# A graph network on one core: the first edge loop re-staged, and a row copy by three 16-bit products

## What is computed

```python
h = relu(layernorm(x)); hw = h @ W.T                     # layer 0, per node
att = leaky_relu(score_src[src] + score_dst[dst])        # per edge and head
x = x + segment_sum(att * hw[src], dst)
h = relu(layernorm(x))                                   # layer 1
z = concat([h[row], h[col], edge_attr]) @ [W_weight, W_gate] + bias
x = x + segment_sum(relu(z_message) * sigmoid(z_gate), row)   # row = src, col = dst
```

## Time and profile before

| what | value |
|---|---|
| time, median of three runs | 5444.96 us (5443.28 to 5455.56) |
| span of the profiled execution | 6861.6 us |
| gather loop in the profile, with its lead-in | 224 to 3233 us |
| second pass over the nodes | 3233 to 3360 us |
| scatter loop in the profile | 3360 to 5950 us |
| third edge loop and final sums | 5950 to 6862 us |

### The profile page before, as it was taken

How to read it: one execution, slowest core, us unless ns; L and a number is a source line. 1 busy time by engine, 2 the same in 40 slices (tenths; PEclk the granted TensorE clock), 3 DMA queues, 4 the chain that set the end, 5 groups by cost and what they waited for, 6 DMA issues and landing times.

```text
span 6861.6 us, 115174 instructions
## 1 busy us (share of the span) xinstructions
PE 4604.1 (67%) x31443; PEld 3550.2 (52%) x31443; DVE 3197.0 (47%) x6951; ACT 1985.4 (29%) x4132; POOL 3725.5 (54%) x3908
## 2 busy tenths in 40 slices
PE   6355555555555555555888878788877878688883
PEld 3244444444444433444566666666666666566663
DVE  7455555555555555566511111112111112399996
ACT  3011111111111111112522222222222222388883
POOL 5654555555555555462366666666666666544442
PEclk8666676676667766677988888888888888899997
DMA  4222222222222222222644444444444444599998
GB/s 144 50 54 50 56 54 53 50 55 52 53 52 54 53 51 52 52 59 56 230 138 138 136 137 137 139 136 140 136 138 137 137 138 141 183 323 325 326 323 313
DMA packets 457998, 866.29 MB, mean 126 GB/s; under 512 B 122766, under 2 KB 276056, under 8 KB 457700
## 3 DMA queue, kind: packets, MB, share of 16 engines
q1 hardware_dynamic: 215031, 439.00, 21.0%
q0 software_dynamic: 177312, 379.95, 19.8%
q10 hardware_dynamic: 65620, 46.95, 2.1%
HBM read 558.92 MB, written 313.00 MB: 127 GB/s over the span
## 4 chain that ended last, share of the span: by engine, by line
PE 39%; issue 19%; DVE 18%; another core or an unknown queue 15%; DMA 6%; ACT 1%; DVEq 1%; SPq 1%; ACTq 0%; POOL 0%; POOLq 0%
PE ps L842 13%; PE ps L840 13%; DMA rows<-parts 5%; PE ps L827 3%; DVE msg L1443 3%; DVE hot L1333 3%; DVE to_node L1317 3%; PE ps L764 2%; PE ps L707 2%; DVE gat L1548 1%; PE ps L675 1%; DVE run_parts L1425 1%; DVE picked L1413 1%; PE ps L720 1%
## 5 line engine op out<-in xcount | busy, mean ns | idle before, releaser
L602 POOL DMA_INDIRECT parts<-rows,sidx x1664 | 1640.5, 986 | 952.9 <-issue 510.6
L1313 DVE TENSOR_SCALAR to_edge<-ps,iota_p 128x1024 bf16<-128x1024 f32 (+1 forms) x417 | 535.3, 1284 | 2084.1 <-remote 1726.7
L842 PE MATMUL ps<-nodes_w,to_edge 128*128 128x256 f32 x3328 | 1117.5, 411 | 231.1 <-issue 226.0
L840 PE MATMUL ps<-w_edge,gat 128*128 128x256 f32 x3328 | 1108.4, 407 | 217.6 <-issue 212.6
L584 POOL DMA_INDIRECT gat<-table,sidx x832 | 859.7, 1033 | 715.9 <-DVE sidx L1325 466.4
L764 PE MATMUL ps<-msg,to_node 128*128 128x128 f32 x3328 | 691.2, 367 | 827.0 <-issue 535.6
L584 POOL DMA_INDIRECT rows<-table,sidx x832 | 793.5, 954 | 663.8 <-DVE sidx L1325 388.2
L764 PEld LDWEIGHTS ps<-msg,to_node 128*128 128x128 f32 x3328 | 609.0, 270 | 883.7 <-issue 883.1
L840 PEld LDWEIGHTS ps<-w_edge,gat 128*128 128x128 f32 x3328 | 675.1, 204 | 431.2 <-issue 328.5
L842 PEld LDWEIGHTS ps<-nodes_w,to_edge 128*128 128x128 f32 x3328 | 677.0, 205 | 416.0 <-issue 324.7
L1044 ACT ACTIVATE rows<-ps 128x512 f32<-128x512 f32 x832 | 466.7, 604 | 1385.8 <-remote 694.8
(11 more groups left out here) (231 smaller groups left out, 6574.3 us busy)
## 6 DMA issues: line engine op xcount, KB each, us to landing
rows<-parts SPq DMA_DIRECT2D x208, 1028.0 KB, 7.5
ea<-in_edge_attr SPq DMA_DIRECT2D x422, 256.0 KB
nodes_w<-table_b SPq DMA_DIRECT2D x208, 128.0 KB
parts<-rows,sidx POOLq DMA_INDIRECT x1664
nodes_w<-table_a SPq DMA_DIRECT2D x416, 64.0 KB, 5.1
gat<-table,sidx POOLq DMA_INDIRECT x832
rows<-table,sidx POOLq DMA_INDIRECT x832
x1w<-x ACTq DMA_DIRECT2D x208, 64.0 KB
```

Of the source, the lines that this page charges most:

```text
L602: nc.gpsimd.indirect_dma_start(out=parts, out_offset=bass.IndirectOffsetOnAxis(ap=sidx[:, s, j:j + 1], axis=0), in_=rows[:, s, j, :], in_o ...
L840: pe.matmul(z, eat[:, s % 2, j // 4, (j % 4) * P:(j % 4 + 1) * P], w_edge[:], start=True, stop=False)
L842: mmi = pe.matmul(z, to_edge[:, s % 2, j * P:(j + 1) * P], nodes_w[:, s, :], start=False, stop=True)
L1313: return nc.vector.tensor_scalar(to, spread.rearrange("p b n -> p (b n)"), iota_p[:], None, ALU.is_equal)
```

## The change

In the first edge loop TensorE's step q takes the work of one step in two halves. Ahead of a wait for `dve0` (VectorE has reduced the scores of group q) stand `turn_keys(q)` and `find_places(q - 1)`, behind it `sum_messages(q - 1)`, `expand_scores(q + 1)`, `spread_rel` and `match_keys(q)`. The places go to the free half of bank 7, where the counts are. VectorE's step q makes the messages of group q itself (before: q - 1), and adds the sums of q - 2 (before: q - 1). ScalarE's queue stores the window of q - 2 at the start of step q and loads that of q - 1 behind its first two evictions. In the scatter loop the window of `table_b` is cut, two steps ahead, into three bf16 parts that add up to it (ScalarE makes the first and the second, VectorE the rest and the third), the one-hot matrix is written in bf16, and three bf16 products take the place of the fp32 one.

```diff
-        SCORES = F + J * B
+        SCORES = F
+        places = ps[:, 7, J * B:2 * J * B]
...
+        b_parts = hot[:, :, 0:3 * 2 * F].rearrange("p s (k f) -> p s k f", k=3)
+        b_rest = hot_t[:].rearrange("p a j n -> p (a j n)").bitcast(F32)[:, 0:2 * 2 * F].rearrange("p (r f) -> p r f", r=2)
+        to_edge_h = [to_edge[:, k, :].bitcast(BF16)[:, 0:GE] for k in range(2)]
...
                 pe.wait_ge(earlier_up, 2 * q + 2)
                 for j in range(J):
-                    at = ps[:, 4, F + j * B:F + (j + 1) * B]
+                    at = places[:, j * B:(j + 1) * B]
                     pe.matmul(at, hot_t[:, s % 2, j, :], digits[:, s % 2, j, :], start=True, stop=False)
                     mmi = pe.matmul(at, earlier[:, j, :], ones_b[:], start=False, stop=True)
-                return mmi
+                mmi.then_inc(places_ps, 1)
...
             def sum_messages(s, q):
                 pe.wait_ge(to_node0, q + 1)
                 pe.wait_ge(copied0, q + 2)
-                pe.wait_ge(msgs0, q + 1)
-                out_ps = ps[:, 4, 0:F]
                 for j in range(J):
-                    mmi = pe.matmul(out_ps, to_node[:, s % 2, j * P:(j + 1) * P],
+                    mmi = pe.matmul(ps[:, 4, 0:F], to_node[:, s % 2, j * P:(j + 1) * P],
                                     msg[:, s % 2, j * F:(j + 1) * F], start=(j == 0), stop=(j == J - 1))
+                return mmi
+
+            def expand_scores(s, q, turn):
+                pe.wait_ge(to_edge_up[0], q + 1)
+                pe.wait_ge(sdw_in[s], 16 * (turn + 1))
+                for j in range(J):
+                    mmi = pe.matmul(ps[:, 4, SCORES + j * 3 * HEADS:SCORES + (j + 1) * 3 * HEADS],
+                                    to_edge_b[:, j * P:(j + 1) * P], sdw[:, s, :], start=True, stop=True)
+                mmi.then_inc(expanded, 1)
...
-            def by_dst_step(s, q, i, turn, w, first):
-
+            def by_dst_step(s, q, i, turn, first, last):
+                pe.wait_ge(digits_up, q + 1)
+                pe.wait_ge(picked_up, q + 1)
+                turn_keys(s, q)
                 if s > 0 or not first:
-                    pe.wait_ge(digits_up, q)
-                    turn_keys((s - 1) % U, q - 1)
-                    sum_messages((s - 1) % U, q - 1)
-                    if s > 1 or not first:
-                        pe.wait_ge(picked_up, q)
-                        find_places((s - 2) % U, q - 2)
-                pe.wait_ge(to_edge_up[0], q + 1)
-                pe.wait_ge(sdw_in[s], 16 * (turn + 1))
...
-                spread_rel(0, i, s + 1)
+                    find_places((s - 1) % U, q - 1)
+                pe.wait_ge(dve0, 3 * q + 1)
                 if s > 0 or not first:
-                    match_keys((s - 1) % U, q - 1)
+                    summed = sum_messages((s - 1) % U, q - 1)
+                    if last and s == U - 1:
+                        summed.then_inc(last_ps, 1)
+                if s < U - 1 or not last:
+                    expand_scores((s + 1) % U, q + 1, turn if s < U - 1 else turn + 1)
+                if s < U - 2 or not last:
+                    spread_rel(0, i, s + 2)
+                match_keys(s, q)
...
-            def edge_products(s, q, f, i, turn):
+            def edge_products(s, q, f, i):
                 pe.wait_ge(to_edge_up[1], f + 1)
                 spread_rel(1, i, s + 1)
-                pe.wait_ge(bw_in[s], 16 * (turn + 1))
+                pe.wait_ge(part_act, 2 * q + 2)
+                pe.wait_ge(part_dve, 2 * q + 2)
                 pe.wait_ge(ea_t, 2 * q + 4)
                 for k in range(4):
                     pe.wait_ge(part_up, 4 * q + k + 1)
...
                         z = ps[:, 4 + k, (j % 2) * 2 * F:(j % 2 + 1) * 2 * F]
                         pe.matmul(z, eat[:, s % 2, j // 4, (j % 4) * P:(j % 4 + 1) * P], w_edge[:],
                                   start=True, stop=False)
-                        mmi = pe.matmul(z, to_edge[:, s % 2, j * P:(j + 1) * P], nodes_w[:, s, :],
-                                        start=False, stop=True)
+                        for part in range(3):
+                            mmi = pe.matmul(z, to_edge_h[s % 2][:, j * P:(j + 1) * P], b_parts[:, s, part, :],
+                                            start=False, stop=(part == 2))
...
+            def store_window(q, g):
+                act.wait_ge(copied0, q + 3)
...
+                act.dma_start(x1[bass.ds(first, P), :], x1o[:]).then_inc(x1_st, 16)
+
+            def load_window(q, g):
+                act.wait_ge(x1_st, 16 * (q + 1))
...
+                act.dma_start(x1w[:], x1[bass.ds(first, P), :]).then_inc(x1_in, 16)
+
+            def by_dst_step(s, q, g, first):
+                if s > 1 or not first:
+                    store_window(q - 2, g - 2)
...
+                if s > 0 or not first:
+                    load_window(q - 1, g - 1)
...
+            def first_part(s, q, turn):
+                act.wait_ge(bw_in[s], 16 * (turn + 1))
+                nc.scalar.activation(b_parts[:, s, 0, :], nodes_w[:, s, :], ACT.Copy).then_inc(part_act, 1)
+
+            def second_part(s, q):
+                act.wait_ge(part_dve, 2 * q + 1)
+                nc.scalar.activation(b_parts[:, s, 1, :], b_rest[:, s % 2, :], ACT.Copy).then_inc(part_act, 1)
+
+            def evict_rows(s, q, turn, last):
+                ahead = s < U - 2 or not last
+                if ahead:
+                    first_part((s + 2) % U, q + 2, turn if s < U - 2 else turn + 1)
...
+                    if k == 1 and ahead:
+                        second_part((s + 2) % U, q + 2)
...
+                dve.wait_ge(places_ps, q + 1)
+                dve.wait_ge(pos_up, q + 1)
...
-            def by_dst_step(v, q, g, turn, w, first):
-
-                f = q + w
+            def by_dst_step(v, q, g, turn, w, first, last):
                 s = v % U
-                last = v > 0 or not first
-                if last:
-                    messages((v - 1) % V, q - 1, turn if v > 0 else turn - 1)
-                    dve.wait_ge(msgs0, q)
-                    next_gather((v - 1) % V, g - 1 + V)
-                dve.wait_ge(spread_up[0], f + 1)
-                by_node(to_edge_b).then_inc(to_edge_up[0], 1)
-                relative(0, dst_of(g + 1), g + 1, s + 1)
-                if last:
-                    dve.wait_ge(keys_ps, q)
-                    split_run((s - 1) % U, q - 1, w)
-                one_hot(s, g).then_inc(hot_up, 1)
-                dve.wait_ge(rel_up[0], f + 1)
-                dve.wait_ge(copied0, q + 1)
+                dve.wait_ge(expanded, U + q + 1)
+                if v > 1 or not first:
+                    add_sums(q - 2)
+                messages(v, q, turn)
+                dve.wait_ge(msgs0, q + 1)
+                next_gather(v, g + V)
+                if v < V - 1 or not last:
+                    dve.wait_ge(spread_up[0], q + 2)
+                    by_node(to_edge_b).then_inc(to_edge_up[0], 1)
+                    relative(0, dst_of(g + 1), g + 1, s + 1)
+                dve.wait_ge(keys_ps, q + 1)
+                if v > 0 or not first:
+                    dve.wait_ge(places_ps, q)
+                split_run(s, q, w)
+                if v > 0 or not first:
+                    pick((s - 1) % U, q - 1, g - 1)
+                if v < V - 1 or not last:
+                    one_hot((s + 1) % U, g + 1).then_inc(hot_up, 1)
+                dve.wait_ge(rel_up[0], q + 1)
                 by_edge(s, iota_ps).then_inc(to_node0, 1)
...
+                for k in range(2):
+                    dve.wait_ge(last_ps, 2 * w + k + 1)
+                    add_sums(q - 2 + k)
...
+            def first_rest(s, q, turn):
+                dve.wait_ge(bw_in[s], 16 * (turn + 1))
+                dve.wait_ge(part_act, 2 * q + 1)
+                nc.vector.tensor_tensor(b_rest[:, s % 2, :], nodes_w[:, s, :], b_parts[:, s, 0, :],
+                                        ALU.subtract).then_inc(part_dve, 1)
+
+            def third_part(s, q):
+                dve.wait_ge(part_act, 2 * q + 2)
+                nc.vector.tensor_tensor(b_parts[:, s, 2, :], b_rest[:, s % 2, :], b_parts[:, s, 1, :],
+                                        ALU.subtract).then_inc(part_dve, 1)
...
+                if ahead:
+                    dve.wait_ge(part_dve, 2 * q + 4)
+                    first_rest((s + 2) % U, q + 2, turn if s < U - 2 else turn + 1)
+                dve.wait_ge(spread_up[1], f + 2)
+                dve.wait_ge(z1_up, 4 * U + 4 * q)
+                by_node(to_edge_h[(s + 1) % 2]).then_inc(to_edge_up[1], 1)
+                if ahead:
+                    third_part((s + 2) % U, q + 2)
```

More of the change, by code:

```diff
@@ L1054, in _ @@
                         evict_turned(s + 1, q + 1)
-                        evict_rows(s, q, turn)
+                        evict_rows(s, q, turn, False)
                 turn = act.snap(w * GU + GU - 1)
@@ new lines, in scatter_step @@
```

(28 more changed lines are left out.)

138 lines of the change are left out of this document (56 added, 82 removed).

## The result

| | before | changed |
|---|---|---|
| median | 5447.22 us (20 runs) | 5456.19 us (20 runs) |
| lowest | 5442.25 us | 5446.23 us |
| highest | 5455.56 us | 5501.94 us |

The ratio is 1.0018, with a 95% interval of 1.0010 to 1.0025: the changed kernel is some 9 us slower (5 to 14), less than the 0.2% that the prediction named as the limit of what can be told. It is inside the range, 5 us above the predicted 5451.

What follows compares the result with a forecast made beforehand. GpSimd's indirect DMAs were taken to bound both edge loops, hiding the rest; 4.1 us at the gather loop's end plus 2.2 at the scatter loop's start made 6.3 on 5445, so 5451 us, range 5439 to 5467.

Steps and rivals of the forecast that it cites:

- GpSimd's pace: Both edge loops: GpSimd's indirect DMAs set the timed pace, 10.1 us a gather step, 10.3 a scatter step; chance 0.83.
- the uncovered ends: Gather loop's end and scatter loop's start, not hidden by GpSimd: together +6.3 us, bounds +1 to +13.
- The bound: Both edge loops: GpSimd paces them; VectorE needs 8.2 us a gather step, TensorE 8.3 a scatter step, 7.4 after the change.
- The rebuilt 5461 or 5493 us: Whole kernel before, rebuilt as if GpSimd never waited; the higher sum counts the first gather's long 65.8 us; 5445 was measured.
- The re-staged loop, the parts, the products: nothing: Both edge loops: new order, copies and subtractions, and bf16 products (0.32 us for three) hidden under GpSimd's pace, priced nothing.
- The end of the gather loop: +4.1: Last scores to SyncE's next DMA: 13.0 us for 8.9, by a second addition, load and store; +4.1 us, bounds 1.3 and 8.
- The start of the scatter loop: +2.2: First product waits for the parts of group 0, so GpSimd's first scatter is 2.2 us later; bounds 0 and 5.
- TensorE as the bound of the scatter loop: Scatter loop: TensorE, not GpSimd, is last, so the products save 183 us, 5262 us; chance 0.08.
- TensorE's issue by records: Timed loops go by TensorE's instruction records, 84 to 100 a scatter step: 408 us slower, 5853 us; chance 0.05.
- VectorE's subtractions: Scatter loop: two-operand SBUF subtractions block GpSimd for their full length, +179 us, 5631 us; chance 0.04.
- by the page it would be 5631: Scatter loop: the skill page on SBUF contention, read as VectorE's two-input subtractions holding up GpSimd's indirect DMAs, giving 5631 us.
- the profiled loop could grow to 3083 us: Profiled scatter loop: if the stalls are the recording's and go by records, from 2590 up to 3083 us, the time unchanged.

Runs made afterwards that it cites:

- e5: Kernel before with GpSimd relieved: five of eight gathers a step, four plain DMAs in place of eight scatters, so work is left out; 4698.53 us, ratio 0.8626.
- e6: Changed kernel with GpSimd relieved: five of eight gathers a step, four plain DMAs in place of eight scatters, so work is left out; 4521.81 us, ratio 0.8303.
- the second recording: The kernel before, unedited, profiled once more; ratio 0.9998 (0.9989 to 1.0007), span 5451.7 us.
- e2: Kernel before with the re-staged first loop alone, the scatter loop keeping the fp32 product; ratio 1.0015 (1.0006 to 1.0024).
- e3: Kernel before with the parts and three bf16 products alone, the first loop as before; ratio 1.0003 (0.9994 to 1.0012).
- e4: Changed kernel with the sums of group 206 added right behind split_run of group 207, ahead of the last two picks; ratio 1.0014 (1.0005 to 1.0023).
- e11: e4 with ScalarE reading the window's index into its register ahead of the wait, for store and load of x1; ratio 1.0012 (1.0003 to 1.0021).
- e7: Kernel before with four more 128x256 fp32 subtractions a step on VectorE in the scatter loop, both operands in SBUF; ratio 1.0067 (1.0050 to 1.0084).
- e8: Kernel before with a one-operand 128x416 reduction, then a two-operand 128x1024 fp32 subtraction, added each scatter-loop step on VectorE; ratio 1.0228 (1.0211 to 1.0245).
- e10: Changed kernel with a one-operand 128x416 reduction on VectorE behind the second subtraction of each scatter-loop step; ratio 1.0019 (1.0010 to 1.0029).

## Why the prediction came out as it did

The mechanism is the one that was forecast, GpSimd's pace over both loops and the loss at the uncovered ends. Three terms were off in size, and partly cancel.

**The bound.** Shown right: GpSimd's pace in both loops, gathers on average 1.254 to 1.259 us apart and scatters 1.288 to 1.292 in every undisturbed recording of a kernel with eight DMAs a step and nothing added on VectorE; and e5 and e6 show the next bounds where the prediction put them (8.2 us for VectorE; 8.3 and 7.4 for TensorE against 8.20 and 7.39). The rebuilt 5461 or 5493 us were high because the rows of the stalled recording were: the first slot at 243.1 in place of 229.1, and the first gather's 65.8 us, 1.1 in the changed kernel. With 229.1 the same sum is 5447, the measured median, but that it fits so well is in part luck. Beside the 5451.7 us of the second recording the sum has the last scores 7 us late (1.26 us a gather for 1.254), the way from there to the first scatter 2 us short, the scatters 3 us long, and the last stretch, which moves by 15 us between recordings, 13 us short.

**The re-staged loop, the parts, the products: nothing.** Right for the loop and the products: e2's gathers take 0.2 us more in all than those of before, and in e6 three bf16 products take 0.33 us (3002.07 to 3002.40) where the sum had 0.32. The parts are not quite nothing: the scatters take 1.5 us longer than before, and 1.1 of it are the 12 collisions with the subtractions (1.1 of 1.8 in e3, 1.9 of 2.5 in e4).

**The end of the gather loop: +4.1.** This term was mis-sized: +5.9. The place and the mechanism were right. To the first addition it is 7.0 us where the sum had 6.5. From there to the load's issue it is 3.4 us where the sum had 2.4, the load takes 1.8 to the second addition for 1.7, and from that to SyncE's DMA it is 2.8 for 2.4: 1.9 us more in all, 14.9 for 13.0. The sum took its 2.4 us from the earlier trace rows, where ScalarE had the window's index in its register and issued the store 0.68 us behind the addition (0.32 in the second recording). In the changed kernel ScalarE reads the index behind the wait, and the issue comes after 1.06 us, twice, and once more it reads it ahead of the load. e11 shows 0.53 us of that for one store.

**The start of the scatter loop: +2.2.** Mis-sized the other way: +1.0 in the changed kernel, +1.5 in e3. The kernel before takes 6.9 us here in the second recording and not 6.35 as in the first. A copy into bf16 is 0.42 us and not 0.36, a smaller error against it.

Together +5.9 and +1.0, +1.5 in the scatters, and -0.9 in a node pass that no edit touches: 7.5 us between the two traces up to the last scatter (the gathers start 0.4 us later and take 0.4 less), where 6.3 were predicted and 9 (5 to 14) measured. The two mis-sized ends, +1.8 and -1.2, partly cancel in the predicted sum.

**The rivals.** TensorE as the bound of the scatter loop: out, e3 gives 1.0003 and not 0.966; e5 and e6 show that it becomes true where GpSimd is relieved, with steps of 8.20 and 7.39 us. TensorE's issue by records: out, by the two spans. VectorE's subtractions: the mechanism that the prediction gave 0.04 exists, the price of 179 us doesn't. (On the 5445 us that the other rivals start from it would be 5624, not 5631.) The argument against it was a row that could not decide: in the earlier trace rows L1425 ends at 1089.93, 0.10 us behind the gather's start, and 0.10 is less than the 0.12 from which a remainder costs. Another pair of the same recording would have shown it:

```profile
2945.41 0.42 DVE L1425 TENSOR_TENSOR run_parts<-run,masks 128x256 int32<-128x256 int32 x1
...
2945.59 1.08 POOL L584 DMA_INDIRECT rows<-table,sidx  x1 [0.30 <-issue]
```

With 0.24 us left the gather takes 1.08 us and not 0.96; it is the longest of its line in the earlier trace rows. In the second recording of before 21 gathers start with more than 0.13 us of L1425 left, and 19 take longer, by up to 0.22. The change escapes by its place: its second subtraction ends at 3403.60 and the next scatter starts at 3403.83 (timeline of the changed kernel):

```profile
3402.54 0.98 POOL L607 DMA_INDIRECT parts<-rows,sidx  x1 [0.30 <-ACT rows L1081]
3403.19 0.41 DVE L1553 TENSOR_TENSOR hot<-hot_t,hot 128x256 bf16<-128x256 f32 x1
...
3403.83 0.98 POOL L607 DMA_INDIRECT parts<-rows,sidx  x1 [0.30 <-issue]
```

VectorE is released by the landing of a scatter (1453 us of its idle time in the loop end with one), so it stands in step with GpSimd, and in nearly every step the subtractions fall in the same place. The Trainium skill, "SBUF — State Buffer", § Who interferes with whom, says that the order of issue and not the shape of the operation decides who blocks; e7 and e8 agree, as a subtraction that comes first stretches the scatter and one that comes later doesn't. The section also infers that `tensor_tensor` leaves the generation of a DMA's descriptors alone, so the prediction's "by the page it would be 5631" goes further than the page does; there e7 and e8 differ from the page, with up to 1.01 us on one scatter, and the measurement decides.

**What the prediction left open.** It said that the profiled loop could grow to 3083 us if the stalls go by records. The changed kernel's recording wasn't stalled, so this was not tested, and what stalled TensorE in the one recording of before stays open.

## What to carry to other kernels

First ask which engine paces the loop in the timed runs. When a profiled span is far above the time, rebuild the time from the steady engine's start-to-start distance, and record once more where that can be had. Work taken off an engine under that pace is worth nothing in the loop, and what the new order leaves behind at the loop's ends is paid in full, one hand-over and register load at a time. And a VectorE instruction with two operands in SBUF beside GpSimd's indirect DMAs is free or costs its remainder, by where it lies when the DMA starts: read its place from the timeline before setting a price.

## What was not expected of the hardware

An indirect DMA of GpSimd that starts while VectorE runs an instruction with two operands in SBUF takes longer by what that instruction has left, less some 0.13 us (0.33 left, 0.20 longer; 0.69 left, 0.57 longer; the longest scatter of e8 took 2.00 us and not 0.98). It is so for fp32 operands beside scatters and for the int32 ones of L1425 beside gathers, and not for e10's reduction of one operand. A scatter that has started isn't touched: of the 204 in e7 that a subtraction only follows, none is over 0.013 us longer than the median. Nor are the ten in e7 that start 0.002 to 0.015 us behind a subtraction's start. One recording of thirteen showed a span 1417 us above the kernel's median, with TensorE idle between its own matmuls; the others end 1.6 to 3.1 us below their own times. In the recordings of e5 and e6 the first gather takes 55.7 and 55.6 us, long like the 65.8 of the earlier trace rows, and in the ten others 1.1; why isn't known.
